# The first stage in another order: modulation columns and first rows ahead of the gate rows

## The reference

```
mod = (silu(c) @ wmod).reshape(2, 6, 1, 256)        # per batch: sa, ca, ga, sb, cb, gb
ga  = (2*(ga >= 0) - 1) * maximum(abs(ga), 0.25)    # gate, guarded away from zero
h   = layernorm(x) * (1 + ca) + sa
q, k, v = h @ Wq + bq, h @ Wk + bk, h @ Wv + bv     # then causal attention in 8 blocks of 256
x   = x + ga * attention(q, k, v)
```

## Time and profile before

| | us |
|---|---|
| median of 3 runs | 1431.72 |
| lowest and highest | 1431.06, 1433.06 |
| the profiled execution | 1432.02 |
| its span | 1430.3 |
| TensorE busy | 1278.1 |
| VectorE busy | 815.8 |
| ScalarE busy | 583.6 |
| GpSimd busy | 482.1 |

### The profile page before, as it was taken

One profiled execution on the slowest core, in us unless ns is written; L12 is line 12 of the kernel. 1 busy time (PEld: TensorE's weight loads), 2 busy tenths in 40 slices (PEclk: granted clock), 3 DMA queues, 4 the chain that ended last, 5 costly groups with the idle time before them and its releaser, 6 DMA issues. The chain is left out here.

```text
span 1430.3 us, 18524 instructions
## 1 busy us (share of the span) xinstructions
PE 1278.1 (89%) x6040; PEld 883.5 (62%) x6040; DVE 815.8 (57%) x1759; ACT 583.6 (41%) x1092; POOL 482.1 (34%) x338
## 2 busy tenths in 40 slices
PE   4999759999999999999997869999988579989897
PEld 4866648888888788888886712233222247868565
DVE  4455564444444444444457577777774557878545
ACT  1322233333333333333333715666677253434342
POOL 2200236556556555556553610111111032122100
PEclk9999669999999999999999957999999888999689
DMA  4010124443343333343330540223310201110001
GB/s 145 1 45 1 57 58 117 112 119 103 103 118 113 98 109 103 110 117 106 103 92 1 176 140 3 61 75 87 74 21 16 83 0 47 43 44 12 0 0 60
DMA packets 49437, 102.68 MB, mean 72 GB/s; under 512 B 8788, under 2 KB 21844, under 8 KB 49372
## 3 DMA queue, kind: packets, MB, share of 16 engines
q1 hardware_dynamic: 49372, 101.87, 24.9%
HBM read 88.52 MB, written 8.93 MB: 68 GB/s over the span
## 5 line engine op out<-in xcount | busy, mean ns | idle before, releaser
L919 DVE TENSOR_TENSOR d_prod<-d_silu,ps 128x512 f32<-128x512 f32 x132 | 90.8, 688 | 247.1 <-ACT d_silu L874 244.0
L1397 DVE CUSTOM_DVE_ANT_0 parts<-ps,causal 128x128 f32<-128x128 f32 (+7 forms) x256 | 183.2, 756 | 51.7 <-PE ps L1303 44.8
L967 POOL TENSOR_TENSOR d_inter<-d_prod,d_wbc 128x512 f32<-128x512 f32 x132 | 200.0, 1529 | 21.0 <-DVE d_prod L919 15.0
L957 POOL TENSOR_TENSOR d_w_lo<-raw,d_w_hi 128x768 fp32r<-128x768 f32 x66 | 121.6, 1843 | 227.3 <-ACT d_w_hi L850 227.3
L911 DVE TENSOR_TENSOR d_i_lo<-d_inter,d_i_hi 128x512 fp32r<-128x512 f32 x132 | 154.6, 1171 | 63.7 <-ACT d_i_hi L856 63.7
L784 PE MATMUL ps<-h_hi,d_w_hi 128*128 128x512 f32 x528 | 166.6, 396 | 5.3 <-POOL d_w_lo L957 4.5
L784 PE MATMUL ps<-h_lo,d_w_hi 128*128 128x512 f32 x528 | 166.1, 395 | 0.0
L784 PE MATMUL ps<-h_hi,d_w_lo 128*128 128x512 f32 x528 | 166.0, 395 | 0.0
L1377 ACT ACTIVATE xn<-ps 128x512 f32<-128x512 f32 (+3 forms) x256 | 114.2, 508 | 93.4 <-PE ps L1320 90.6
L850 ACT CAST d_w_hi<-raw 128x768 fp32r<-128x768 f32 x66 | 54.9, 833 | 198.2 <-PE ps L797 197.0
L1303 PE MATMUL ps<-qk 96*128 96x512 bf16 (+3 forms) x288 | 89.6, 382 | 32.3 <-DVE hmax L1397 21.8
(11 more groups left out here) (260 smaller groups left out, 2201.8 us busy)
## 6 DMA issues: line engine op xcount, KB each, us to landing
d_wbc<-router_weights_t SPq DMA_DIRECT2D x132, 256.0 KB, 3.8
raw<-in_moe SPq DMA_DIRECT2D x66, 384.0 KB, 4.2
qk<-qk_parts SPq DMA_DIRECT2D x72, 128.0 KB, 2.7
qk_parts<-parts SPq DMA_DIRECT2D x16, 384.0 KB, 2.8
raw<-in_mlp SPq DMA_DIRECT2D x16, 384.0 KB, 3.1
h_t<-qk_parts SPq DMA_DIRECT2D x24, 128.0 KB, 2.7
x_tok<-in_x SPq DMA_DIRECT2D x4, 512.0 KB, 8.4
h_hi<-raw SPq DMA_DIRECT2D x32, 64.0 KB, 2.3
```

Source lines behind the costliest of these rows:

```text
L919: nc.vector.tensor_tensor(prod[:, s % 3, :], sg[:, s % 3, :], ps[:, 2 * (s % 2) + 1, :], ALU.mult).then_inc(s_t, 1)
L957: nc.gpsimd.tensor_tensor(w_lo[:, slot, :], raw[:, slot, :], w_hi[:, slot, :].bitcast(F32), ALU.subtract).then_inc(s_wlo, 1)
L967: nc.gpsimd.tensor_tensor(inter[:, s % 3, :], prod[:, s % 3, :], wbc[:, s // 2, (s % 2) * GW:(s % 2 + 1) * GW], ALU.mult).then_inc(s_int, 1)
L1397: nc.vector.tensor_tensor_reduce(masked[:, at % 3, 0:k], ps[:, bank:bank + 2, :].rearrange("p a n -> p (a n)")[:, 0:k], causal[:, SEQ - k: ...
```

## The change

In the first block only:

- VectorE: the statistics and rows of group 0 come first, then the modulation columns, then the statistics and the rows of group 1, then the gate rows, then `cbf`. In the loop the rows of g+2 are made right after their statistics, so VectorE waits there for GpSimd's `rstd` of the same group.
- GpSimd: `rstd` of group 1 goes behind `wqkv_lo`; in the loop `low_h(g)` stands ahead of `rstd` of g+2.
- TensorE: the transposes of group 0 stand between the modulation columns and the gate matmuls. The waits for `s_modd` and for the weights are no longer ahead of them (ScalarE still waits for `s_modd`).
- Banks: the columns go to bank 6 and the gate matmuls to bank 7, which are free until v of group 0; v of group 0 waits for `s_cb`, which VectorE raises after it has read both.

```
@@ vector @@
+                    dve.wait_ge(s_x[0], 16)
+                    ln_stats(0, link)
+                    ln_rows(dve, 0, s_ln, 0)
+                    dve.wait_ge(s_modp, 1)
+                    mod_finish(0, link, ps[:, 6, 0:24], (0,)).then_inc(s_modd, 1)
+                    dve.wait_ge(s_x[1], 16)
+                    ln_stats(1, link)
+                    ln_rows(dve, 1, s_ln, 0)
+                    dve.wait_ge(s_modp, 2)
+                    link(nc.vector.tensor_copy(ga[:, :, :], ps[:, 7, :].rearrange("p (b d) -> p b d", b=BATCH)))
+                    guard(ga[:, :, :], (gat[:, 0], gat[:, 1]), link)
                     dve.wait_ge(s_const, 16)
                     nc.vector.tensor_copy(cbf[:, :], consts[:, 0:384]).then_inc(s_cb, 1)
-                    dve.wait_ge(s_x[0], 16)
-                    ln_stats(0, link)
-                    dve.wait_ge(s_x[1], 16)
-                    ln_stats(1, link)
-                    ln_rows(dve, 0, s_ln, 0)
-                    dve.wait_ge(s_modp, 1)
-                    link(nc.vector.tensor_copy(ga[:, :, :], ps[:, 1, :].rearrange("p (b d) -> p b d", b=BATCH)))
-                    guard(ga[:, :, :], (gat[:, 0], gat[:, 1]), link)
-                    mod_finish(0, link, ps[:, 0, 0:24], (0,)).then_inc(s_modd, 1)
                     dve.wait_ge(s_bias, 48)
                     for g in range(NG):
                         if g + 2 < NG:
                             dve.wait_ge(s_x[g + 2], 16)
                             ln_stats(g + 2, link)
-                        if g + 1 < NG:
-                            ln_rows(dve, g + 1, s_ln, 0)
+                            ln_rows(dve, g + 2, s_ln, 0)
@@ gpsimd @@
-                    ln_pool(pool, 0, range(2))
+                    ln_pool(pool, 0, range(1))
                     pool.wait_ge(s_whi, 1)
                     nc.gpsimd.tensor_tensor(wq_lo[:, :, :, :], wqkv[:, :, :, :], wq_hi[:, :, :, :].bitcast(F32),
                                             ALU.subtract).then_inc(s_wlo, 1)
+                    ln_pool(pool, 0, (1,))
                     for g in range(NG):
+                        low_h(pool, g, s_h).then_inc(s_hlo, 1)
                         if g + 2 < NG:
                             ln_pool(pool, 0, (g + 2,))
-                        low_h(pool, g, s_h).then_inc(s_hlo, 1)
@@ tensor @@
-                    mod_columns(0, wmod, ps[:, 0, 0:24], range(6))
+                    mod_columns(0, wmod, ps[:, 6, 0:24], range(6)).then_inc(s_modp, 1)
+                    pe.wait_ge(s_const, 16)
+                    pe.wait_ge(s_ln, 1)
+                    ln_transposes(0, 0).then_inc(s_lnt, 1)
                     pe.wait_ge(s_crep, 1)
                     for b in range(BATCH):
                         for k in range(KC):
-                            last = nc.tensor.matmul(ps[:, 1, b * D:(b + 1) * D], crep[:, b, k, :],
+                            last = nc.tensor.matmul(ps[:, 7, b * D:(b + 1) * D], crep[:, b, k, :],
...
                     last.then_inc(s_modp, 1)
-                    pe.wait_ge(s_modd, 1)
-                    pe.wait_ge(s_const, 16)
                     pe.wait_ge(s_wqkv, 48)
                     pe.wait_ge(s_wlo, 1)
-                    pe.wait_ge(s_ln, 1)
-                    ln_transposes(0, 0).then_inc(s_lnt, 1)
...
                             if g:
                                 pe.wait_ge(s_pev_d, 4 * (g - 1) + 2 + m + 1)
+                            else:
+                                pe.wait_ge(s_cb, 1)
```

More of the change, by code:

```diff
@@ L327, in _ @@
                                 .then_inc(s_pev_d, 1)
-                    dve.wait_ge(s_modp, 2)
+                    dve.wait_ge(s_modp, 3)
                     mod_finish(0, link, ps[:, 0, 0:24], (1,))
```

## The result

The changed kernel took 1422.75 us (median of 4 runs, 1421.69 to 1424.06), the kernel before, on the same chip, 1431.51 (4 runs, 1431.06 to 1433.06). The ratio is 0.9936, with a 95% interval of 0.9923 to 0.9948: 8.8 us between the medians, or 0.6% faster. The forecast was 1419.7, with 1418.7 to 1420.7 as its own range. The measured median lies 3 us above it and outside that range; it is 0.15 above the upper end of the wide one (1422.6), and the ratio times the 1431.72 that the prediction started from gives 1422.6, that end itself. The direction and the path came out as forecast, the gain was smaller than the 12.0 expected.

A forecast was written before the change was run, and what follows sets the result against it. The first stage's start was taken as set by VectorE's order, then its pace by TensorE. Third group at 40.05 for 51.98 gains 11.9; 1432.02 - 12.0 = 1420.0, against the median 1419.7 us; range 1418.7 to 1420.7, wide 1416.2 to 1422.6.

The forecast's parts named there:

- the wide one: The wider range for the whole kernel's time, 1416.2 to 1422.6 us, covering the rows not being held and most of Rival B.
- Head of the stage: First stage up to the first projection: it starts at 18.6 in place of 29.02, 10.4 us earlier.
- the held columns cost TensorE nothing here: Before the first projection: columns held to 15.65, but ScalarE's modulation and TensorE's gate matmuls both end near 18.5 to 18.6.
- The hold: VectorE's rows (L133) stand still beside GpSimd's low_h: group 1's rows end at 22.1, group 2's at 31.9.
- Rival A: First stage: VectorE's rows are not held by GpSimd; gain 14.2 us, 1417.5 us in all; chance 0.20.
- The new wait: First group: k's eviction queues behind held rows until 32.6; TensorE waits 2.3 to 2.8 us, third group starts at 40.05.
- TensorE's clock: First projections: a slow start of 0.5 us in place of 2.51, mattering little since k's eviction sets the third group's start.
- Rival B: First stage: the wait for k also drops TensorE's clock, 2 to 3 us more, 1422.2 us; chance 0.11.
- The term of the base: Kernel before, first group of projections: 11.81 us against 9.30 at full speed, 2.51 more, with a slow start.
- Afterwards, in the stage: Later groups: group 3's rows held until near 41.2, k of group 1 evicted by 41.9; 0 to 0.5 us lost.
- Afterwards, behind the stage: Stages after the first keep their length, so what the first stage gains, the kernel gains.
- The 0.7 us that the range allowed for the spread: Allowance for the spread of runs, used with the upper-bound gain of 14.8 us to set the range's lower end, 1416.2.

The follow-up runs named there:

- k first: Changed kernel, but VectorE's loop evicts k of group g ahead of the rows of group g+2; 1417.44 and 1419.98 us in two sets.
- guard late: Changed kernel, but VectorE's guard of the gate rows is moved to after the evictions of group 1; 1419.64 us, ratio 0.9911.
- the fillers: Changed kernel plus ten throw-away matmuls on TensorE ahead of its wait for k's eviction; 1421.53 us, ratio 0.9920.
- both edits: Changed kernel with k's eviction ahead of the rows of g+2 and the gate rows' guard moved later; 1419.18 us, ratio 0.9918.

## Why the prediction came out as it did

- *Head of the stage*: right, step by step. Tokens in at 5.45, rows at 8.67, L198 held until 14.86 (14.85 forecast), columns at 15.67 (15.65), first projection at 18.63 (18.6). The gate matmuls took 2.76, 3.62 and 3.62 us in the three profiles (3.76 forecast) and were fully covered: TensorE then waited 1.5, 0.6 and 0.7 us for ScalarE, which had waited for the columns until 15.70. So "the held columns cost TensorE nothing here" was too strong. By these waits, and as an estimate, the projections could have started up to that much earlier without the hold; no run tried it.
- *The hold*: right. Rows of group 1 end at 22.16 (22.1), those of group 2 at 32.02 (31.9). Rival A did not occur in any profile in which the two met: one row of L133 took 2.36 to 2.61 us beside an uncut `low_h`, where it takes 0.40 alone. That is not what the rule in the Trainium skill, page "SBUF — State Buffer", section "Who interferes with whom", gives if L133 is outside the two-port modes. That it is outside them was inferred from its speed alone; no run here tests it, so what it is in the rule or in the reading that fails stays open.
- *The new wait*: right in place and size. 2.18 us (2.3 to 2.8), TensorE going on at 32.73 (32.6), and the third group at 40.17 and 40.23 (40.05) in the two profiles of the changed kernel in which the clock held. k first removed it, and guard late cut it to 0.4, in two different ways.
- *TensorE's clock*: here the forecast was short. It took the new wait to cost nothing but its own length. Rival B had 0.11; the clock fell in one of three profiles of the changed kernel, with 1.6 us lost (2 to 3 were priced). The evidence against it was a wait of 2.03 us at 1.00 in another stage, and a wait of that length goes both ways. In the profiles of k first and of the fillers the clock held, and it held in two of three of the changed kernel too.
- *The term of the base*: the 2.51 us of slow start in the kernel before were taken as its price. Its second profile had 10.73 - 9.30 = 1.43. So 1.1 us of the 12.0 were this one execution's, or 0.5 against the mean of both. After the change the first group takes 9.89, which is 0.59 over 9.30: `cbf` is 0.52 of it (the rows of k first and of both edits show it), and the slow start 0.07, where 0.5 was forecast.
- *Afterwards, in the stage*: the rows of group 3 were expected to be held by `low_h(2)` until near 41.2, without cost. They were not held (1.39 at 37.58), since `low_h(2)` begins only at 40.21; there was more margin than thought, and the sum does not change by it.
- *Afterwards, behind the stage*: no stage behind the first was expected to change. The rest varied from 1352.2 to 1358.6 over the fourteen profiles, 1356.0 and 1358.5 for the kernel before, and 1355.0 to 1358.4 for the changed one. The 1.8 us that the first pair of profiles shows as given back are within that, and go with the granted clock; no profile ties them to the change. The 0.7 us that the range allowed for the spread were too few. That the median came to the very end of the range is in part luck: with four runs it depends on how many of them caught a low stretch.

Together: mean score stage before (74.34 + 72.82) / 2 = 73.6, after (63.82 + 62.16 + 62.22) / 3 = 62.7. That is 10.9 us from the first stage, where 12.0 was forecast. The three sets of runs gave ratios that are worth 9.2 to 10.6 us. The step that came out short is the paragraph on TensorE's clock ("It matters little"), by two terms of about the same size: the slow start of the kernel before, 2.51 in the forecast and 1.97 as the mean of two profiles, and the low clock behind the new wait, nothing in the forecast and 1.6 in one of three profiles, 0.5 on average. Together they are the 1.1. That the second comes from the wait is likely by the count above, and not shown.

A version that is better than both is k first: 0.9904 and 0.9918 of the kernel before, 4.3 us below the changed kernel in one set and 2.3 in the other, where the first stage explains 2.3 to 3.9. The intervals of the ratios overlap with the changed kernel's, so its lead over the changed kernel rests on the profiles of the first stage more than on the times.

## What to carry to other kernels

Moving a producer forward pays in full only as far as the next queue lets it: here the rows that were made earlier stood ahead of an eviction that TensorE needed, and putting the eviction first was worth a further 2.3 us, and with it went a wait behind which the clock may fall. Before a VectorE operation is placed behind a wait for GpSimd, look at what GpSimd does next: here its next instruction was ready, and VectorE's row was held for the whole of it. When a hold seems unchanged by an edit, look at the single instructions: the sum of the four rows hid that one of them had got through. A term read from a single profile that contains a slow start carries an error of a us, and a second profile of the kernel before would have shown it.

## What the runs showed of the hardware

- VectorE's rows are held an instruction of GpSimd at a time. Beside an uncut `low_h` (2.38 us) one row took 2.46; beside its two halves (1.29 and 1.32) one row took 1.37 and the next 1.36, each ending 0.15 us after its half. In guard late the first row began 0.17 us ahead of `low_h` and took 0.41, and the second was held for 2.50.
- A small instruction of VectorE is held as well: one on 128x4 took 1.85 us beside `wqkv_lo`, where it takes 0.17 alone.
- Of six profiles in which TensorE waited 1.6 to 2.6 us at a time, three have the lower clock behind a wait; a wait of 2.2 us was followed by it in two profiles and not in three. Where it fell in the changed kernel, the four pairs of matmuls behind the wait took 0.86 to 1.05 us where 0.63 is full speed, and the third group came 1.6 us later.
- Before the change the gate matmuls (8 of 256 columns) took 3.76 us, after it 2.76, 3.62 and 3.62. In the new place they come behind the transposes, and the last of them ran at the higher level: the shortest takes 0.38 us, where all took 0.63 or more before. The first pair of projections behind them took 0.70 us where it had taken 1.22. The granted clock is given as 1.00 in both profiles there, so the durations tell the level and that column does not.
